# A two-layer decoder on one core: contexts in a ring of six loaded at the start, keys of phases one and three stacked in a step of their own, and new tables for the order

## What is computed

```python
x = x + L0_attn(layernorm(x))                 # phase 0: causal linear attention, 16 heads
x = x + L0_xattn(layernorm(x), ctx, ctx, mask)  # phase 1: attention over 512 context rows, 16 heads
x = x + L0_ffn(layernorm(x))                  # 8 experts, the best two of them
x = x + L1_attn(layernorm(x))                 # phase 2: causal, window of 128, 16 heads
x = x + L1_xattn(layernorm(x), ctx, ctx)      # phase 3: two softmaxes over 512 context rows, 8 heads,
                                              #          with a layer norm, a ffn and a layer norm inside
x = x + L1_ffn(layernorm(x))                  # ternary weights, gelu
```

## Time and profile before

| | us |
|---|---|
| median of 3 runs | 942.75 |
| lowest, highest of them | 939.88, 949.34 |
| the profiled execution, its own time | 939.69 |
| its span, first to last instruction | 937.8 |

### The profile page before, as it was taken

One profiled execution on the slowest core, in us unless ns is written; L12 is line 12 of the kernel. 1 busy time (PEld: TensorE's weight loads), 2 busy tenths in 40 slices (PEclk: granted clock), 3 DMA queues, 4 the chain that ended last, 5 costly groups with the idle time before them and its releaser, 6 DMA issues.

```text
span 937.8 us, 19032 instructions
## 1 busy us (share of the span) xinstructions
PE 790.6 (84%) x6202; PEld 430.8 (46%) x6202; DVE 663.9 (71%) x2253; ACT 481.4 (51%) x998; POOL 342.6 (37%) x888
## 2 busy tenths in 40 slices
PE   2588669999998798977979999989999996887864
PEld 1246323443444354545655654454444453544543
DVE  4868747889878686837769868868787885766220
ACT  3323235655565466644646566455655663564631
POOL 6984302122134443434434442132223434413232
PEclk9779979999999899979999999999999999999985
DMA  6498830412035554636454414354424418622000
GB/s 216 90 211 169 190 53 5 61 37 44 5 76 134 108 132 64 139 53 122 97 114 100 89 32 75 56 121 72 93 71 76 88 38 156 113 59 27 7 6 6
DMA packets 124961, 79.79 MB, mean 85 GB/s; under 512 B 8312, under 2 KB 122176, under 8 KB 124736
## 3 DMA queue, kind: packets, MB, share of 16 engines
q1 hardware_dynamic: 124864, 78.59, 41.3%
HBM read 43.99 MB, written 32.90 MB: 82 GB/s over the span
## 4 chain that ended last, share of the span: by engine, by line
PE 58%; DVE 17%; issue 7%; DMA 6%; POOL 5%; ACT 4%; SPq 2%; DVEq 0%; POOLq 0%; ACTq 0%
PE ob L1277 10%; PE mb L1215 8%; PE eb L1243 5%; PE eb L1244 5%; PE side L1127 3%; PE side L1136 3%; PE side L1144 3%; DMA cT<-ctxT_dram 3%; DVE junk L1715 3%; PE eb L1238 2%; DVE mx L1723 2%; DMA QW<-mrow 2%; PE eb L1240 2%; PE eb L1247 2%; PE side L1053 2%
## 5 line engine op out<-in xcount | busy, mean ns | idle before, releaser
L1439 ACT ACTIVATE probs<-eb 128x512 f32<-128x512 f32 (+1 forms) x512 | 274.5, 568 | 211.0 <-PE eb L1244 103.5
L1715 DVE CUSTOM_DVE_ANT_0 junk<-mb,maskq_add 128x512 bf16<-128x512 f32 x256 | 168.8, 688 | 38.2 <-PE mb L1215 32.8
L1277 PE MATMUL ob<-probs,V 128*32 128x256 f32 (+1 forms) x2048 | 130.2, 372 | 3.3 <-ACT probs L1439 3.3
L1034 POOL TENSOR_SCALAR nm<-mx 128x8 bf16<-128x8 f32 x80 | 19.9, 248 | 245.6 <-DVE mx L1715 139.3
L1243 PE MATMUL eb<-maskk_add,identb 128*128 128x512 bf16 x256 | 98.3, 384 | 9.7 <-issue 8.2
L1723 DVE TENSOR_REDUCE mx<-mb 128x1 f32<-128x512 f32 x128 | 83.7, 685 | 27.0 <-PE mb L1215 25.3
L1215 PE MATMUL mb<-KS,QP 128*128 128x512 bf16 x256 | 90.6, 387 | 9.4 <-DVE mx L1715 9.2
L1244 PE MATMUL eb<-QP,KS 128*128 128x512 bf16 x256 | 98.0, 383 | 0.0
L943 POOL TENSOR_SCALAR rstd<-mv 128x2 f32<-128x2 f32 x64 | 17.0, 266 | 198.4 <-DVE mv L1502 197.1
L1277 PEld LDWEIGHTS ob<-probs,V 128*32 128x32 f32 x2048 | 54.0, 109 | 62.9 <-issue 29.6
L1317 ACT ACTIVATE hn<-X,nshift,rstd 128x128 f32<-128x128 f32 x80 | 35.0, 485 | 52.0 <-POOL nshift L950 51.8
(11 more groups left out here) (194 smaller groups left out, 1647.6 us busy)
## 6 DMA issues: line engine op xcount, KB each, us to landing
QP<-bounce SPq DMA_DIRECT2D x48, 256.0 KB, 5.5
KS<-bounce SPq DMA_DIRECT2D x32, 384.0 KB, 8.5
bounce<-scratch SPq DMA_DIRECT2D x48, 192.0 KB, 2.3
bounce<-scratch SPq DMA_DIRECT2D x64, 128.0 KB, 2.2
KS<-bounce SPq DMA_DIRECT2D x32, 192.0 KB, 5.7
bounce<-scratch SPq DMA_DIRECT2D x16, 384.0 KB, 2.6
cT<-ctxT_dram SPq DMA_DIRECT2D x16, 256.0 KB, 6.1
bounce<-scratch SPq DMA_DIRECT2D x16, 256.0 KB, 4.4
```

What stands on the lines that cost most here:

```text
L1277: ins = nc.tensor.matmul(bank[32 * j:32 * j + 32, S - n:S], v_of(core, kt, 4 * g + j), pr[:, (j % 2) * n:(j % 2 + 1) * n], start=(first_ a ...
L1439: nc.scalar.activation(probs[:, u % PROBS, 0:n], eb[:, u % 2, 0:n], ACT.Exp, scale=SCALE[core.p]).then_inc(probs_by[1], 1)
L1715: ins = V_.tensor_tensor_reduce(junk[:, e.n % 2, :], bank, maskq_add[:, t, :], 1.0, NEG_EXP, ALU.add, ALU.max, mx[slot][:, t, h:h + 1])
```

## The change

1. **Contexts in a ring.** Six buffers cT (CTXS = 6) in place of three. All contexts of sequences 0 to 5 are loaded at the start, behind the x of all sequences, which move ahead of the third weight load; sequences 6 and 7 come into the buffers of 0 and 1 in a new last step "next ctx" of the runs to3.0 and to3.1. Phase 3 uses what phase 1 used: 8 loads in place of 16. The tile `tern` goes; the ternary weights' scratch lies in QW0, so the first stack into QW0 waits for them.
2. **Keys stacked as a step of their own.** Spreads of queries and of keys have a semaphore each. In phases 1 and 3 a step "k stack" waits for the keys' spreads and the slot and issues the two KS DMAs; "stack" then waits for the queries' spreads and issues the two or three of QP or QW. In phases 0 and 2 "stack" issues both, keys first.
3. **Other tables.** EARLY is 4 for 12, URGENT, LATER, AFTER and RANK are others, and so are assumed landing times. The lists of all engines come out otherwise.

```diff
-LANES, SLOTS, WIDES, OUTS, OB, QN, MROWS = 3, 3, 2, 3, 1, 3, 4
+LANES, SLOTS, WIDES, OUTS, OB, QN, MROWS, CTXS = 3, 3, 2, 3, 1, 3, 4, 6
...
-STACK_LANDS = (5.7, 8.5, 5.7, 8.0)
-ACTIVE, EARLY = 4, 12
+STACK_LANDS, K_LANDS = (5.7, 5.7, 5.7, 5.7), 6.5
+ACTIVE, EARLY = 4, 4
...
-    return steps + [("sp", "stack", 3.3 if p == 3 else 2.65, last)]
-CTX_STEPS = [("sp", "ctx load", 0.6, ()), ("pe", "ctx", 1.03, ("ctx load",)), ...
+            steps += [..., ("sp", "k stack", 1.35, ("k spread 0", "k spread 1", "values"))]
+    steps += [("sp", "stack", (2.65, 1.35, 2.65, 2.0)[p], last)]
+    return steps + [("sp", "next ctx", 0.6, ("values",))] if p == 3 else steps
...
-RANK = {"turn": -1, "nm": 0, "row": -1, "chain": 0.4, "keep": 0.6, "chain on TensorE": 1.5, "max": 2, "exp": 3, "av": 4}
+RANK = {"turn": -1, "nm": 0, "row": -1, "chain": 0, "keep": 4.3, "chain on TensorE": 1.5, "max": 2, "exp": 2.0, "av": 4}
...
-        cT = sbs(LANES, "cT", [P, SK])
+        cT = sbs(CTXS, "cT", [P, SK])
...
-        tern = sb("tern", [P, 2, FF])
+        tern = QW[0][:].rearrange("p h q -> p (h q)").bitcast(F32).rearrange("p (i n) -> p i n", i=2)
...
             load_w(3)
             load_w(1)
-            load_x(3)
+            for b in range(3, B):
+                load_x(b)
+            for b in range(CTXS):
+                load_ctx(b)
             load_w(2)
             sp.dma_start(ebias[:], experts_bias).then_inc(ebias_in, 16)
-            for b in range(4, B):
-                load_x(b)
...
+            def keys_stacked(run, back):
+                core, l, n = run.new, run.lane, KEYS[run.new.p]
+                sp.wait_ge(k_spread[l], 16 * PARTS * (N_TAKES(run) + 1))
+                sp.wait_ge(slot_init, core.slot + 1)
+                slot_emptied(sp, run)
+                for r in range(2):
+                    if core.p == 3:
+                        sp.dma_start(KS[core.slot][64 * r:64 * r + HALF_ROWS, :, 0:SK], back[...]).then_inc(stack_in[core.slot], 16)
+                    else:
+                        sp.dma_start(KS[core.slot][64 * r:64 * r + HALF_ROWS, :, 0:n], back[...]).then_inc(stack_in[core.slot], 16)
...
-                    yield "ctx load"
-                    last = run_before(run, ("to1", "to3"))
-                    if last:
-                        sp.wait_ge(lane_free[l], N_RUNS(last) + 1)
-                    sp.dma_start(cT[l][:], ctxT[run.b:run.b + 1].rearrange("o p t -> p (o t)")).then_inc(ctx_in[l], 16)
...
+                if p in (1, 3):
+                    yield "k stack"
+                    keys_stacked(run, back)
                 yield "stack"
-                sp.wait_ge(bounce_in[l], 16 * 2 * PARTS * (N_TAKES(run) + 1))
+                if p in (0, 2):
+                    keys_stacked(run, back)
+                sp.wait_ge(q_spread[l], 16 * PARTS * (N_TAKES(run) + 1))
+                if p == 3 and core.wide == 0 and not WIDE_BEFORE[core]:
+                    sp.wait_ge(ternary_ready, 1)
...
+                    yield "next ctx"
+                    if run.b + CTXS < B:
+                        sp.wait_ge(lane_free[l], N_RUNS(run) + 1)
+                        load_ctx(run.b + CTXS)
```

More of the change, by code:

```diff
@@ L226, in chain_ready @@
             return False
-        if name == "ctx load":
-            return True
+        if name == "ctx" and ctx_landed[run.b] > t:
+            return False
         if run.name == "end" and name == "turned 1" and made.get(f"ternary {TERNARY - 1}", never) > t:
             return False
-        if name in ("ctx", "outputs", "stats") and lane_free[run.lane] > t or name == "stats" and run.name == "to0" and t < X_LANDS[min(run.b, 2)]:
+        if name in ("ctx", "outputs", "stats") and lane_free[run.lane] > t or name == "stats" and run.name == "to0" and t < X_LAND[run.b]:
             return False
@@ L241, in chain_ready @@
             return min(query_free) <= t
+        if name == "k stack":
+            return made.get(f"queries {run.new.slot}", never) <= t
         if name == "stack":
@@ L353, in plan @@
                     run.at[name] = end + SPREAD_LANDS
-                elif name == "ctx load":
-                    run.at[name] = end + CTX_LANDS
+                elif name == "next ctx" and run.b + CTXS < B:
+                    ctx_landed[run.b + CTXS] = end + CTX_LANDS
                 elif name == "stack":
@@ L359, in plan @@
                         wide_users[run.new.wide].append(run.new)
-                    run.new.stacked = end + STACK_LANDS[run.new.p]
+                    run.new.stacked = max(end + STACK_LANDS[run.new.p], run.at.get("k stack", 0.0) + K_LANDS)
                     stacked.append(run.new)
@@ L783, in queries @@
                     sp.wait_ge(q_part[run.lane], N_TAKES(run) * PARTS + (a + 1))
-                    spread(run.lane, a, Q_OF, 0, S)
+                    spread(run.lane, a, Q_OF, 0, S, q_spread)
             def keys(run, parts_):
@@ L1154, in chain_steps @@
                     yield "ctx"
-                    pe.wait_ge(ctx_in[l], 16 * (N_CTX(run) + 1))
-                    nc.tensor.matmul(side[:, l, :], w(f"k{PHASE_OF[name]}"), cT[l][:], start=True, stop=True).then_inc(filled[l], 1)
+                    if run.b < CTXS:
+                        pe.wait_ge(ctx_in, 16 * CTXS)
+                    else:
+                        pe.wait_ge(ctx_late[run.b - CTXS], 16)
+                    nc.tensor.matmul(side[:, l, :], w(f"k{PHASE_OF[name]}"), cT[run.b % CTXS][:], start=True, stop=True).then_inc(filled[l], 1)
                     yield from finish(run, PHASE_OF[name] - 1)
```

55 lines of the change are left out of this document (30 added, 25 removed).

## The result

| us | before | after |
|---|---|---|
| median of 4 runs | 943.2 | 902.56 |
| lowest, highest | 939.88, 949.34 | 898.67, 911.18 |
| profiled execution, own time (span) | 939.69 (937.8) | 900.44 (898.7) |

After over before is 0.9571, with a 95% interval of 0.9524 to 0.9618: 40.6 us faster. The prediction had 922 us, so the direction and the range (902 to 938) hold, the range by 0.6 us only. The size was about half: 21 us forecast, 40.6 measured, outside the forecast's own 910 to 930.

The account below looks back on a forecast made before the run. TensorE was taken as the bound from 130 to 280 and 520 to 760 us, loads, transfers and an end chain elsewhere; -8 -4 -3 -1 -6 -3 +4 = -21 gave 918.7 us, 922 us as median, range 902 to 938 us.

Parts of the forecast that it names:

- Keys stacked ahead: Stacks of phases 1 and 3: keys' issue time, 1.3 us per core, hidden under the queries' landing; 1 us, bounds 0 to 10.
- The 8.19 us at the first row stay: TensorE's wait ahead of 124.40 us, for the first row of maxima, remains, as the row is again behind a whole stack.
- First chains, -8: Start: sequence 2 third removes VectorE's 9.48 us wait for x and shortens GpSimd's selects; 8 us off, bounds 5.9 to 9.5.
- The loads ahead: Start: six contexts of 256 KB added fall where DMA engines are empty; cost nothing, up to 3 us if they collide.
- Fewer loads later, -4 and -3: Four context loads fewer from 44 to 125 us, 4 us off; TensorE's 3.19 us wait for a context gone, 3 us.
- Rows, -6: Phase 3: TensorE's three waits for rows of maxima, 11.6 us, shrink by 6 us, bounds 0 to 11.6.
- The order, -3 and +4: New list: 2.7's late stack gets more work ahead, 3 us off; 3.3, 3.5 and 3.6 get less, 4 us on.
- The split gives nothing: Rival, 30%: rows and stacks wait as before, only the start and the loads gain; 14 us off, 929 us.
- Phase 3 and the start run full: Rival, 17%: new tables bring 280 to 480 us to the steady rate, 760 to 880 us halves its idle; 897 us.
- Slower: Rival, 7%: phase 3 stacks come too late at first maxima of 3.3, 3.5, 3.6 and 3.7, 7 us each; 957 us.
- the tail: Last 58 us, one chain after the last core: left at 58 us; over 62 us would show the prediction wrong.
- 130 to 280 us busy for under 97%: Sign of being wrong: TensorE, busy 146.6 of 150 us in this stretch before, falls below that share.

Follow-up runs that it names:

- Experiment 3: Kernel before, lists kept, keys and queries given a semaphore each, keys' DMAs sent inside the stack step once their spreads landed: 0.9753, 922.7 us.
- experiment 9: Kernel before, lists kept, stack DMAs keys first, then queries, but sent only when the queries' spreads have landed too: 0.9896, 935.05 us.
- experiment 4: Kernel before with only EARLY, URGENT, LATER, AFTER and RANK of the kernel after, order made anew: 1.0092, 952.89 us.
- Experiment 12: The kernel after, unchanged, run and traced once more: 0.9578, 905.0 us.
- experiment 10: Kernel before, lists kept, only contexts changed: six loaded at the start, 6 and 7 at their own step, none for phase 3: 0.9918, 937.18 us.
- experiment 11: Kernel after with sixteen idle DRAM-to-DRAM copies of 256 KB added, one at each first spread of keys of phases 1 and 3: 0.9558, 903.12 us.
- Experiment 5: Kernel after, lists kept, keys' DMAs put back in the "stack" step behind any row between, own semaphore kept: 0.9663, 910.54 us.
- experiment 6: Kernel before, own lists, with keys split off inside the stack step, x of sequence 4 loaded early, six contexts loaded at the start: 0.9644, 910.65 us.

## Why the prediction came out as it did

**The step that failed** is "Keys stacked ahead": "two issues of 0.62 us move under the landing of the queries' spreads: 1.3 us for each core of phases 1 and 3, on the path only where TensorE runs short of work, in phase 3. I take 1 us in all." Experiment 3 measured the split at 2.5%, or 23 us, on the lists of before. Three things were wrong in that passage.

- *The price.* It is not the issue time of the keys but the time for which they stood waiting for the queries' spreads: 4.6 us for each of two stacks ahead of the first row (experiment 3).
- *The place.* It is on the path up to the first row. There spreads and stacks form a loop: a stack is issued, the next chain's spreads stand behind it, SyncE waits for all of them, the queues run empty, and only then goes the next stack. An average share of 0.93 hid these gaps; experiment 3 ran the same stretch at 1.02.
- *The order.* Keys then queries in place of by turns was taken for nothing and gives 1.0% (experiment 9). With it a whole stack is complete about 0.5 us sooner. Why, was not tried by itself.

The argument from the Trainium skill's page "DMA: Bandwidth & Descriptors" (section "Queues, rings and completion order"), ring order, was applied to the wrong pair. That queries directly behind keys gain nothing may well hold; but the same order puts the spreads behind the previous stack, and by that it speaks for the split. The landings of 6.0 to 9.2 us agree with it.

**"The 8.19 us at the first row stay"** failed with it: 2.51 us after, none in experiment 3. The row still stands behind a whole stack, but the stacks ahead of it have come closer together. The wait came of the periods between stacks, not of what stands directly ahead of the row. By the issues of their keys the last three periods ahead of the row are 12.0, 13.9 and 15.0 us before, 10.7, 9.6 and 11.7 in experiment 3, and 12.7, 15.2 and 10.1 in the kernel after. So the split was shown to shorten them on the old list; on the new one the list has a part in it too, which no run takes apart (experiment 4).

**First chains, -8**: right. The first exponentials came 7 us sooner, qf 7.5 us, between the bounds of 5.9 and 9.5. The selects did become short. But GpSimd paid part of it back: its small operations at 12.03 and 14.79 us take 2.68 and 3.71 us, where the same forms took 0.71 and 0.24 us at 19.50 and 20.29 us before. It is not VectorE's clearing as a whole that stretches them: the short ones before ran beside a MEMSET (19.48 to 21.24 us), and in the trace after the same forms take 0.71 and 0.24 us at 10.32 and 11.12 us beside the MEMSET of 9.89 us. The two long ones overlap a CAST of 128x4096 and end 0.6 and 0.1 us behind its end (14.13 and 18.42 us). The second was begun 1.4 us ahead of its CAST, while the MEMSET directly in front of that ran. The first of the three selects before is the same case: begun at 25.57 us, ahead of a CAST from 26.76 to 28.98 us, it ended at 29.13. Experiment 12's trace repeats the two long ones to 0.01 us; no run took the CASTs away. The loads ahead cost nothing, as said.

**Fewer loads later, -4 and -3**: the sum is near (experiment 10: 7.7 us by the runs), but by luck, as one of its two mechanisms is not there. The 4 us, bytes out of the stretch up to 125 us, are refuted twice: by experiment 10, where 1.0 stays at 124.37 us, and by experiment 11, where four copies of 256 KB more in that stretch, and 4 MB in all, cost nothing. (That kernel's engines still had an idle place to take them: the DMA view of the kernel after is empty from 85 to 87 us.) The lower bound, "0 (if latency and not bytes bounds it)", was the right end. The context wait did go.

**Rows, -6**: right in kind, and somewhat low. No wait of TensorE for a QW row is over 1.6 us in the trace of the kernel after, and none over 2.2 in its second trace. From 3.0's first exponentials to the next phase 1 core's, 176 us became 162, of which TensorE's idle time went from 25.1 to 16.9 us; the other 6 us are TensorE's own busy time, at a granted clock of 0.96 for 0.94. The second trace, with all matmul records, agrees: 144.2 us busy in that stretch at 0.98.

**The order, -3 and +4**: 2.7's wait is gone. The stalls at 3.3, 3.5 and 3.6, whose run-up had become short, didn't come, because the keys' step goes out while SyncE waits for a row. Experiment 5 takes that away and gets them back, at 3.7, 3.5 and 3.6, for 9.3 us. So the worry was right about the lists and wrong about the cover.

**Sum.** With the sizes of the runs (in us of 943): split -23, x in its place -8, contexts -8, together -34 on the lists of before (experiment 6), and -7 or so for the step's place on the new lists. What the prediction lacked is the split: its largest piece stood in the sum with 1 us. That the result still lies inside 902 to 938 us, by 0.6 us (by 3 us in experiment 12), is owed to a low edge that was set for another rival's sake, not to the mechanism.

**The rivals.** "The split gives nothing" (929 us) is refuted by experiment 3. "Phase 3 and the start run full" (897 us) lies nearest to the result, 5.6 us off, but gives it to the new tables; experiments 4, 5 and 6 show that these carry little. "Slower" didn't occur; its mechanism is that of experiment 5, at under 5 us for each core. The steady stretch (153.0 us both times) and the tail (57.7 against 58) came out as said. One sign of being wrong, "130 to 280 us busy for under 97%", reads 144.4 of 150 us (96.3%) in the trace of the kernel after, which lacks 21 matmul records there, and 145.9 (97.3%) in the second trace, which lacks none.

**Open.** What the early sending is worth on the new lists; why stacks with keys first are complete sooner; why experiment 3's gain goes on growing from 11 us at 1.0 to 23 at the end (the two shorter waits for rows are 3.3 us of it); and why pieces that save the same idle time lose or keep it later.

## What to carry to other kernels

Price a DMA that is sent earlier by how long its issuing engine would stand for the neighbours it was bundled with, measured where the queue is loaded, and not by its issue time. A mean busy share of the DMA engines of over 0.9 is no proof that bytes bound a stretch: look at its slices for gaps ahead of each large issue, the mark of a round trip (transfer, semaphore, next issue). And to weigh a mechanism in a kernel whose order a planner makes, hold the lists still and edit them by hand: the tables without the mechanisms cost 0.9%, the mechanisms under the old tables 2.2%, the mechanisms on the old lists gave 3.6%, and the same mechanisms on the new lists, without the step's place, 3.4%.

## What was not expected of the hardware

- Sixteen more copies of 256 KB cost nothing (0.9558 against 0.9578 beside it), though four fell in a stretch with a DMA share of 0.90, whose rate rose from 183 to 198 GB/s.
- The order of four large DMAs in one queue, by turns or two and two, is worth 1.0% of this kernel [0.7 to 1.4%]: the same bytes have all landed after a median of 7.8 us in place of 8.4.
- A MEMSET of VectorE alone leaves GpSimd's operations on 128x2 at 0.71 and 0.24 us; one that was begun during a MEMSET with a CAST of 128x4096 directly behind it took 3.71 us and ended with the CAST.
- A spread of 64 to 384 KB takes two to four times as long to land when some 1.3 MB stand ahead of it in the queue: those of 128 KB a median of 6.5 us from 84 to 120 us, 2.2 us over the whole run. Their landing is what the next issue waits for.
